# Routed experts: the first layer's bias moves from a TensorE product to VectorE

## What is computed

```python
x = x + attention_a(layernorm(x))      # 16 heads of 128
x = x + ffn(layernorm(x))
x = x + attention_b(layernorm(x))      # latent keys and values, rotary
x = x + ffn(layernorm(x))

def ffn(x, gate_w, w1, b1, w2, b2, shared_w1, shared_b1, shared_w2, shared_b2):
    xf = x.reshape(-1, D)                                   # 2048 tokens of 512
    top_logits, top_idx = jax.lax.top_k(xf @ gate_w, 2)     # 2 of 8 experts
    gates = ...                                             # softmax of the two, spread over 8
    h = gelu(jnp.einsum('nd,edh->neh', xf, w1) + b1)        # b1: 8 x 256
    out_e = jnp.einsum('neh,ehd->ned', h, w2) + b2
    routed = jnp.einsum('ne,ned->nd', gates, out_e)
    shared = gelu(xf @ shared_w1 + shared_b1) @ shared_w2 + shared_b2
    return routed + shared
```

## Time and profile before

| | us |
|---|---|
| median of three runs | 2483.08 (2480.66 to 2484.35) |
| the profiled execution | 2484.95 |
| its span, first to last instruction | 2483.1 |
| PE busy | 2356.3 (95%) |
| DVE busy | 1626.9 (66%) |
| ACT busy | 1143.2 (46%) |
| POOL busy | 656.6 (26%) |
| routed tiles, first layer, first to last bias product | 1170.20 to 1328.78 |
| routed tiles, second layer | 2273.23 to 2430.30 |

### The profile page before, as it was taken

One profiled execution on the slowest core, in us unless ns is written; L12 is line 12 of the kernel. 1 busy time (PEld: TensorE's weight loads), 2 busy tenths in 40 slices (PEclk: granted clock), 3 DMA queues, 4 the chain that ended last, 5 costly groups with the idle time before them and its releaser, 6 DMA issues. The chain is left out here.

```text
span 2483.1 us, 41710 instructions
## 1 busy us (share of the span) xinstructions
PE 2356.3 (95%) x13140; PEld 2010.6 (81%) x13140; DVE 1626.9 (66%) x3774; ACT 1143.2 (46%) x2698; POOL 656.6 (26%) x546
## 2 busy tenths in 40 slices
PE   6999999999999999989999789999999999779997
PEld 5888888989898989867787568888888888657885
DVE  7555555455555564675455748988888888865456
ACT  4444444344434353442332436666666666533334
POOL 1111111111101020134221324444444434253223
PEclk9999999999999999988999889999999999999999
DMA  4524233342333425217774100000000000127755
GB/s 165 178 91 173 95 145 121 118 147 105 137 130 111 155 91 196 85 49 254 255 246 170 48 10 10 18 9 18 9 18 9 18 9 9 35 104 245 262 198 228
DMA packets 101107, 277.66 MB, mean 112 GB/s; under 512 B 8896, under 2 KB 9336, under 8 KB 95376
## 3 DMA queue, kind: packets, MB, share of 16 engines
q1 hardware_dynamic: 80144, 220.77, 25.1%
q0 software_dynamic: 11360, 37.76, 3.9%
q10 hardware_dynamic: 9504, 17.85, 2.5%
HBM read 131.34 MB, written 145.00 MB: 111 GB/s over the span
## 5 line engine op out<-in xcount | busy, mean ns | idle before, releaser
L609 DVE SCALAR_TENSOR_TENSOR x<-bank,inv,x 128x512 f32<-128x512 f32 x512 | 361.6, 744 | 173.5 <-PE bank L76 171.5
L619 DVE TENSOR_TENSOR hq_lo<-bank,hq_hi 128x512 fp32r<-128x512 f32 (+1 forms) x320 | 201.3, 637 | 267.2 <-ACT hq_hi L555 102.5
L74 PE MATMUL bank<-xT_hi,w_hi 128*128 128x512 f32 x864 | 350.7, 406 | 17.8 <-POOL w_lo L700 6.4
L497 ACT ACTIVATE s<-s,top 128x128 f32<-128x128 f32 (+3 forms) x512 | 282.1, 553 | 155.9 <-DVE top L601 155.9
L76 PE MATMUL bank<-xT_hi,w_lo 128*128 128x512 f32 x864 | 344.0, 398 | 0.0
L75 PE MATMUL bank<-xT_lo,w_hi 128*128 128x512 f32 x864 | 343.5, 398 | 0.0
L563 ACT ACTIVATE hq_hi<-bank 128x512 fp32r<-128x512 f32 x128 | 76.4, 597 | 388.3 <-PE bank L76 388.3
L74 PE MATMUL bank<-wo_hi,hq_hi 128*128 128x512 f32 (+1 forms) x576 | 233.4, 405 | 2.7 <-issue 1.1
L75 PE MATMUL bank<-wo_lo,hq_hi 128*128 128x512 f32 (+1 forms) x576 | 228.2, 396 | 0.5 <-issue 0.3
L76 PE MATMUL bank<-wo_hi,hq_lo 128*128 128x512 f32 (+1 forms) x576 | 228.2, 396 | 0.4 <-issue 0.2
L601 DVE CUSTOM_DVE_ANT_0 s<-bank,mask 128x128 f32<-128x128 f32 (+3 forms) x512 | 216.7, 480 | 4.3 <-PE bank L76 4.3
(11 more groups left out here) (285 smaller groups left out, 5850.8 us busy)
## 6 DMA issues: line engine op xcount, KB each, us to landing
sorted_x<-blank SPq DMA_DIRECT2D x48, 1584.0 KB, 11.4
arena<-split_w SPq DMA_DIRECT2D x32, 1024.0 KB
split_w<-arena SPq DMA_DIRECT2D x48, 512.0 KB, 3.0
raw<-dram_wr SPq DMA_DIRECT2D x24, 512.0 KB, 5.8
w_raw<-dram_wa SPq DMA_DIRECT2D x16, 512.0 KB, 3.6
arrived<-routed_y SPq DMA_DIRECT2D x8, 1024.0 KB, 8.0
row_pt_hi<-sorted_x ACTq DMA_DIRECT2D x22, 264.0 KB
row_pt_lo<-sorted_x ACTq DMA_DIRECT2D x20, 264.0 KB
```

The lines of the kernel that those rows point to most:

```text
L74: nc.tensor.matmul(out, hi, mov_hi, start=first, stop=False)
L497: nc.scalar.activation(at, at, ACT.Exp, bias=m.top[:, b, t:t + 1], scale=-1.0, accum_out=m.rowsum[:, b, t:t + 1]).then_inc(a.probs_ready, 1)
L609: nc.vector.scalar_tensor_tensor(out=xt, in0=m.bank[6 + t % 2][:, :], scalar=m.inv[:, b, t:t + 1], in1=xt, op0=ALU.mult, op1=ALU.add).then ...
L619: return nc.vector.tensor_tensor(out, bank, hi.bitcast(F32), ALU.subtract).then_inc(done, 1)
```

## The change

The thirteenth product of each routed tile goes. PE now signals after the twelfth. A new step `bias(i, expert)` on DVE adds the bias, read from a row spread over 128 partitions (`m.b1s`), while it moves bank i % 2 to `hs`, and signals `rt.biased`. `gelu(i)` on ACT waits for that and works in place on `hs`. The register load with the expert is taken once a tile, at the head of the loop's body, in front of `bias(i)`; `output(i - 1)` uses the register of the turn before. The split of b1, its two stores and one small load at the start go; the load of two rows per expert becomes a load of one spread row of 256, issued beside that of b2.

```diff
@@ route_up, PE
-        ge(pe, rt.gelu_done, i0 + i - 1)
+        ge(pe, rt.biased, i0 + i - 1)
...
-            product(nc, out, m.xsT[HI][i % 2][:, at], m.xsT[LO][i % 2][:, at], w, wl, k == 0, False)
-        nc.tensor.matmul(out, m.ones[0:2, :], slot[0:2, WCOLS:WCOLS + HF], start=False, stop=True).then_inc(rt.up_done, 1)
+            last = product(nc, out, m.xsT[HI][i % 2][:, at], m.xsT[LO][i % 2][:, at], w, wl, k == 0, k == KD - 1)
+        last.then_inc(rt.up_done, 1)
@@ gelu, ACT
-        act.wait_ge(rt.up_done, i0 + i + 1)
-        ge(act, rt.h_turned, i0 + i - 1)
-        nc.scalar.activation(m.hs[:, i % 2, :], m.bank[i % 2][:, 0:HF], ACT.Gelu).then_inc(rt.gelu_done, 1)
+        act.wait_ge(rt.biased, i0 + i + 1)
+        nc.scalar.activation(m.hs[:, i % 2, :], m.hs[:, i % 2, :], ACT.Gelu).then_inc(rt.gelu_done, 1)
@@ DVE
-    def output(i):
-        expert = dve.value_load(m.tab[0:1, E_AT + i:E_AT + i + 1], min_val=0, max_val=E - 1)
+    def bias(i, expert):
+        dve.wait_ge(rt.up_done, i0 + i + 1)
+        ge(dve, rt.h_turned, i0 + i - 1)
+        nc.vector.tensor_tensor(m.hs[:, i % 2, :], m.bank[i % 2][:, 0:HF],
+                                m.b1s[:, bass.ds(expert % 2, 1), WCOLS:WCOLS + HF].rearrange("p a n -> p (a n)"),
+                                ALU.add).then_inc(rt.biased, 1)
+
+    def output(i, expert):
         dve.wait_ge(rt.y_done, i0 + i + 1)
...
+    before = None
     for i in range(TILES):
+        expert = dve.value_load(m.tab[0:1, E_AT + i:E_AT + i + 1], min_val=0, max_val=E - 1)
+        bias(i, expert)
         if i + 2 < TILES:
             input_lo(i + 2)
             mark(i + 2)
         if i:
-            output(i - 1)
+            output(i - 1, before)
...
         hidden_lo(i)
-    output(TILES - 1)
+        before = expert
+    output(TILES - 1, before)
@@ SP
-        sp.dma_start(m.slots[0:2, s, WCOLS:WCOLS + HF].bitcast(F32), bi[e, :, :]).then_inc(rt.w_ready, 16)
...
     def load_bias(e):
+        sp.dma_start(m.b1s[:, e % 2, WCOLS:WCOLS + HF], b1r[e:e + 1, :].to_broadcast([P, HF])).then_inc(rt.w_ready, 16)
         sp.dma_start(m.b2[:, e % 2, :], bs[e:e + 1, :].to_broadcast([P, D])).then_inc(rt.w_ready, 16)
@@ the split at the start
-            nc.scalar.activation(m.b1hi, m.b1raw, ACT.Copy).then_inc(m.b1_split, 1)
...
-            pool.wait_ge(m.b1_split, 1)
-            nc.gpsimd.tensor_tensor(m.b1lo, m.b1raw, m.b1hi.bitcast(F32), ALU.subtract).then_inc(m.b1_split, 1)
...
-            sp.dma_start(m.b1raw, b1r).then_inc(small_loaded, 16)
...
-                sp.dma_start(bi[:, 0, :], m.b1hi.bitcast(F32)).then_inc(m.bias_stored, 16)
-                sp.dma_start(bi[:, 1, :], m.b1lo.bitcast(F32)).then_inc(m.bias_stored, 16)
```

More of the change, by code:

```diff
@@ L845, in prepare @@
             nc.gpsimd.tensor_copy(m.meta[:, :, 0], m.table[:, TOKEN]).then_inc(m.gw_split, 1)
-            pool.wait_ge(m.b1_split, 1)
-            nc.gpsimd.tensor_tensor(m.b1lo, m.b1raw, m.b1hi.bitcast(F32), ALU.subtract).then_inc(m.b1_split, 1)
-            nc.gpsimd.tensor_tensor(m.b2raw, m.b2raw, m.b2both, ALU.add).then_inc(m.b1_split, 1)
+            nc.gpsimd.tensor_tensor(m.b2raw, m.b2raw, m.b2both, ALU.add).then_inc(m.b2_summed, 1)
     return prepare
-SMALL = 16 * 6
+SMALL = 16 * 5
 def last_head(h):
@@ L1521, in ffn_vector @@
         dve.wait_ge(m.filled, 32 * PIECES)
-        dve.wait_ge(m.bias_stored, 48)
+        dve.wait_ge(m.bias_stored, 16)
     norm_start_vector(nc, dve, m, n, r, 2)
@@ L1696, in load_split, with ffn_sync @@
         sp.dma_start(dst[part].bitcast(F32), src).then_inc(sem, 16)
-def ffn_sync(nc, sp, m, n, f, g, rt, a, L, ws, bi, bs, xs_d, ys_d, between=nothing, after=nothing):
+def ffn_sync(nc, sp, m, n, f, g, rt, a, L, ws, b1r, bs, xs_d, ys_d, between=nothing, after=nothing):
     r, s0, i0 = 2 * L + 1, 2 * B * L, TILES * L
@@ L1735, in ffn_sync @@
     load_split(sp, ws, 2 * E + 2, whole, (m.pt_hi[:, 0:1024], m.pt_lo[:, 0:1024]), f.w1b_in)
-    sp.wait_ge(m.bias_stored, 48)
+    sp.wait_ge(m.bias_stored, 16)
     if L:
@@ L1867, in __init__ @@
         self.up_done = sem("up_done")
+        self.biased = sem("biased")
         self.gelu_done = sem("gelu_done")
@@ L1952, in program @@
         m.slots = arena[:, :].rearrange("p (s n) -> p s n", s=2)
+        m.b1s = full("b1s", "arena", slice(0, 2 * SLOT))[:, :].rearrange("p (s n) -> p s n", s=2)
         m.ckv = [arena[:, i * B * S:(i + 1) * B * S].rearrange("p (b n) -> p b n", b=B) for i in range(2)]
         m.raw_lo, m.prep_hi_t = arena[:, 6144:7168], arena[:, 7168:8192]
-        m.b1hi, m.b1lo = arena[0:E, 4096 + 256:4096 + 512], arena[0:E, 4096 + 512:4096 + 768]
         m.ckv32 = m.s[:, 0:S]
@@ L2024, in program @@
         x0_loaded = [ctx.enter_context(nc.semaphore(f"x0_loaded{t}")) for t in range(NT)]
-        small_loaded, m.gw_split, m.b1_split, stored, m.bias_stored, m.rope_loaded, m.rezeroed = (
-            ctx.enter_context(nc.semaphore(n)) for n in ("small_loaded", "gw_split", "b1_split", "stored", "bias_stored", "rope_loaded", "rezeroed"))
+        small_loaded, m.gw_split, m.b2_summed, stored, m.bias_stored, m.rope_loaded, m.rezeroed = (
+            ctx.enter_context(nc.semaphore(n)) for n in ("small_loaded", "gw_split", "b2_summed", "stored", "bias_stored", "rope_loaded", "rezeroed"))
         m.zeros_set, m.count_set, m.raw_loaded, m.prep_hi, m.prep_lo, m.prep_stored, m.filled = (
             ctx.enter_context(nc.semaphore(n)) for n in ("zeros_set", "count_set", "raw_loaded", "prep_hi", "prep_lo", "prep_stored", "filled"))
-        ws, bi, bs, ys_d = (nc.dram_tensor(n, shape, F32, kind="Internal").ap() for n, shape in (
-            ("split_w", (PIECES, P, 2048)), ("split_b1", (E, 2, HF)), ("sum_b2", (E, D)), ("routed_y", (2 * B * S + TILES * P, D))))
+        ws, bs, ys_d = (nc.dram_tensor(n, shape, F32, kind="Internal").ap() for n, shape in (
+            ("split_w", (PIECES, P, 2048)), ("sum_b2", (E, D)), ("routed_y", (2 * B * S + TILES * P, D))))
         xs_d = [nc.dram_tensor(f"sorted_x{i}", (BLOCKS * P, ROW), F32, kind="Internal").ap() for i in range(2)]
@@ L2060, in store_biases @@
             def store_biases():
-                sp.wait_ge(m.b1_split, 3)
-                sp.dma_start(bi[:, 0, :], m.b1hi.bitcast(F32)).then_inc(m.bias_stored, 16)
-                sp.dma_start(bi[:, 1, :], m.b1lo.bitcast(F32)).then_inc(m.bias_stored, 16)
+                sp.wait_ge(m.b2_summed, 1)
                 sp.dma_start(bs, m.b2raw).then_inc(m.bias_stored, 16)
@@ L2075, in _ @@
             attend_sync(nc, sp, m, a1, False, wa, woa, wva, prepare_sync(sp, m, wr, ws, xs_d), store_biases)
-            ffn_sync(nc, sp, m, n, f, g, rt, a1, 0, ws, bi, bs, xs_d[0], ys_d, load_wkva, load_wqa)
+            ffn_sync(nc, sp, m, n, f, g, rt, a1, 0, ws, b1r, bs, xs_d[0], ys_d, load_wkva, load_wqa)
             sp.wait_ge(rt.combined, 4 * NT)
@@ L2081, in _ @@
             attend_sync(nc, sp, m, a2, True, wb, wob)
-            ffn_sync(nc, sp, m, n, f, g, rt, a2, 1, ws, bi, bs, xs_d[1], ys_d)
+            ffn_sync(nc, sp, m, n, f, g, rt, a2, 1, ws, b1r, bs, xs_d[1], ys_d)
             for b in range(B - 1):
```

1 line of the change is left out of this document (removed).

## The result

The changed kernel takes 2471.20 us in the median of five runs (2468.64 to 2471.54); the kernel before took 2484.35 beside it (2480.66 to 2485.58). The ratio is 0.9943, with a 95% interval of 0.9932 to 0.9954: 13 us faster, where the forecast said 11.5 and 2471.6 (counted from 2483.08, so that the difference of 13 to 11.5 is the fairer comparison). The time is right. The way to it is not, and most of what follows is about that.

What follows compares the result with a forecast made beforehand. PE bounds the routed tiles before; afterwards a DVE and ACT chain of 3.98 us per tile does. Per layer 4.9 + 36 x 3.98 + 3.1 + 1.2 = 152.5 us, 11.5 less in all: 2471.6, range 2461 to 2490.

Steps and rivals of the forecast that it cites:

- The present bound and the uneven tiles: Routed tiles before: PE bounds them at 3.92 us each; DVE's register load adds 0.22 of unevenness, making 4.14.
- The load leaves the slow place: DVE's register load, moved, starts 3.1 us after POOL's previous scatter and so is no longer slow.
- 0.40 for the product: On PE, dropping the bias product saves 0.40 us per tile, at most 31 us, leaving PE 3.52 per tile.
- A closed chain that PE has no part in: Loop over DVE and ACT from `bias` to the next `bias`, 3.98 us per tile, above PE's 3.52.
- `hidden_lo` to the next `bias`: Last link of the chain, in DVE's queue with the register load: 0.87 us, bounds 0.34 and 1.28.
- PE stays the bound: Rival: DVE's queue work is done while `hidden_lo` waits for ACT; chain 3.45, below PE's 3.52; 2439 us; chance 0.10.
- The sum: Routed tiles of both layers: 3.98 us per tile, 152.5 us per layer, 11.5 us less in all.
- the slow load: Rival: one DVE register load in three takes 0.72 us more, 0.24 in the chain, 17 us: 2489; chance 0.12.
- No overlap: Rival: DVE's register load begins only when `hidden_lo` has ended; link 1.28, chain 4.39, 2501 us; chance 0.08.
- a dear load: Rival: DVE's register load takes 0.60 us, making the chain 4.28 and the time 2493; chance 0.02.
- the signs listed: Trace signs of a right forecast: tiles near 3.98 us apart, PE's `route_down` waiting some 0.4 for `hidden_lo` nearly every tile.

Runs made afterwards that it cites:

- before_dve_load_moved: The kernel before, bias product kept, with only DVE's register load moved from behind `ids` to the loop's head: 2479.91 us, ratio 0.9946.
- pe_load_early: The changed kernel with PE's register load for tile i + 1 moved behind `turn(i + 2)`, ahead of the waits for `hidden_lo` and the gelu: 2456.16 us.
- pe_load_behind_down: The changed kernel with PE's register load for tile i + 1 moved between `route_down(i - 1)` and `turn_hidden(i)`: 2458.08 us, ratio 0.9862 to the kernel before.
- dve_load_twice: The changed kernel with DVE's register load made twice ahead of `bias`: 2491.11 us, ratio 0.9991 to the kernel before.
- before_no_bias_load_moved: The kernel before without the bias product (nothing adds the first layer's bias) and with DVE's register load at the loop's head: 2446.26 us, ratio 0.9815.
- The plain store: The kernel before with POOL's indirect scatter of each tile's rows replaced by a plain DMA to a fixed block: 2486.47 us, ratio 0.9975.

## Why the prediction was right in its time and wrong in its reason

- *The present bound and the uneven tiles*: right. With the load out of the way the kernel before runs at 3.92 to 3.95 per tile, and the unevenness was worth 12.9 us. The step that tied it to the load is confirmed by `before_dve_load_moved`.
- *The load leaves the slow place*: right in part, and not the reason for the even tiles. The forecast had it start 0.61 behind `output`'s start with a scatter 3.1 us old; it starts 0.06 behind it, and the scatter is 2.5 us old (median). 23 of 78 loads still take over 400 ns, where 37 did before (median 313 against 362, longest 950 against 1165). The tiles are even because a load that runs under `output` and `hidden_lo` has slack.
- *0.40 for the product*: a little small. On a clear path it was 0.43 per tile, and the new tile without it 3.48 (3.52 forecast).
- *A closed chain that PE has no part in*: this is the step that failed. The prediction wrote "`hidden_lo` to the next `bias`: the same queue work that stood between `ids` and `output`, 0.87". The measured 0.79 to 0.81 looks like it and is another thing: the queue work was done during `output` and `hidden_lo`, the link alone would be 0.40 (`pe_load_early`), and the rest was a wait for PE. The forecast took from the earlier trace rows that a load begins with the instruction just ahead of it in the queue; in the changed kernel it begins one instruction earlier. The bound of 0.34 "if all queue work were hidden" was named, and with it the rival "PE stays the bound" at 2439. The hidden queue work came true, yet not that rival's time, because of the next point.
- *What the prediction never looked at*: PE's own queue. In both kernels PE's register load stands behind `turn_hidden` and can't begin before the gelu has ended. In the kernel before, the gelu ended 1.40 us ahead of `turn_hidden` (1210.97 and 1212.37), and the load was through in time. The change puts `bias` ahead of the gelu and takes the product from PE's work; now the gelu ends 0.56 ahead (1211.09 and 1211.65), and the load comes out of its cover. In the prediction's own terms: the gelu was moved, and what stands in the queue behind those who wait for it was not listed for PE. That cost 18 us (`pe_load_behind_down` against the change) to some 23 (`pe_load_early`).
- *The sum*: 3.98 was forecast and 3.84 to 3.86 measured per tile; 11.5 and 13 us. Two errors stood against each other: a link that was 0.47 too long, and a standstill of 0.36 on PE that was missing. That they nearly cancel, and the time with them, is luck.
- *The rivals*: the slow load stayed in a part of the tiles (23 of 78, longest 950 ns) and was covered by the slack; the rival priced it at 17 us, and it cost nearly nothing here. No overlap and a dear load did not occur; the load's median of 0.31 stands at half of the 600 ns that the Trainium skill, page "DMA: Bandwidth & Descriptors", section "Latency and other measured facts", gives as the floor of a `tensor_load`. With the register instructions behind it, one load does cost 0.6 us of DVE's queue (`dve_load_twice`).
- *What would have shown it*: the signs listed were distance, 0.87, loads near 305, no idle time ahead of `output`, and PE's wait for `hidden_lo`. The distance, the 0.87 and the idle time came out nearly as written, the loads in their median (313) but not in 23 of 78, and only the last spoke clearly against the chain (one wait instead of one per tile). A distance that fits is weak evidence; what the wait ended on decides.

In short: moving DVE's load brings 13 us by itself (`before_dve_load_moved`), and with the bias moved on top of it the gain is 13 to 15. So the removal of the product, worth 33 us on a clear path, and the new `bias` together gave about 2 us at most. (No run moved the bias with DVE's load left in its old place, so the share of the load inside the change is inferred.) Of the 31 or more that were lost, 18 to 23 us are the loop through PE's register load and come back when that load moves; with both loads moved the kernel takes 2453.72 us. 8 us stay lost against the 46.3 of `before_no_bias_load_moved`. By an estimate from the trace, 0.15 us in every second tile, PE's waits for `hidden_lo` are some 6 of them.

## What to carry to other kernels

When an edit makes an operation later, list for every engine that waits for it what stands behind the waiting instruction in its queue, register loads too. They run ahead at no cost until an unmet wait stops the queue; then they begin late, and cost what the work in front no longer covers (0.36 us a tile here). A loop whose computed length fits the measured distance is not yet the right loop; read what each wait in it ended on, and double one link to see whether the distance follows. And part a change that moves two things: one of them alone may bring the whole gain.

## What the runs showed of the hardware

In the changed kernel DVE's load begins 0.06 us behind the start of `output`, with `hidden_lo` still to come; PE's load, behind a wait for the gelu, begins 0.05 us behind the gelu's end in every tile but the first of a layer. DVE's load costs 0.3 us and its register instruction 0.19; doubled, 0.6 us came to the queue, and 0.19 us to the tile.
- A register load on PE or DVE takes 295 to 315 ns in most tiles, or up to 1260 in some. What goes with a slow one (over 400 ns) is the time since the start of POOL's last scatter, whichever engine loads. Over the loads of PE and DVE in all kernels with the scatter (1872, both layers), 129 of the 143 that began 1.3 to 1.9 us behind a scatter's start were slow, 164 of 467 at 1.9 to 2.6 us, and 42 of the other 1262. In `pe_load_early` PE's load begins 1.3 to 2.4 us behind the scatter in 63 of 76 tiles and has a median of 409 ns; moved behind `route_down`, where it mostly begins within the first 0.6 us, the same load has 301.
- What causes it stays open. The plain store showed that indirect addressing is not needed for it. The loads of the tiles' rows, which ACT issues some 0.76 us ahead of DVE's load in the kernel before, are not needed either: of the 16 of DVE's loads that came over 4 us behind the last of them, 8 were slow, of the other 62, 29. A run without any store in that place wasn't tried.
